# Rows added, measured and normalized, and projection weights mixed, inside the first convolution's edge pass

## The chip, the cores and the metric

One core of a Trainium2 chip runs one program that computes the whole network. The metric is the device time of one execution in microseconds, median of several runs. The engines are TensorE (PE, with its weight load PEld), VectorE (DVE), ScalarE (ACT), GpSimd (POOL) and SyncE (SP, which here only issues DMAs).

## What is computed

A graph has 6250 nodes with 256 features and 100000 edges, sorted by destination. First a graph convolution is added to the input and the rows are normalized; then three attention layers with weights by node type and edge type run over the same edges.

```python
h = x @ W
norm = deg_inv_sqrt[src] * deg_inv_sqrt[dst]
out = segment_sum(h[src] * norm[:, None], dst)         # first convolution
x = layernorm(x + out)                                 # rows of the node stage
# attention, layer 0 of 3: K, V, Q of each node, by node type; keys also by edge type
Q = typed(x, W_Q, node_type); K = typed(x, W_K, node_type); V = typed(x, W_V, node_type)
kt = typed(K[src], W_E, edge_type); scores = sum(Q[dst] * kt) / sqrt(HD) * mu.T[edge_type]
```

## The kernel before

The nodes are 50 windows of 128, of which 49 (`FILLED`) hold nodes. The edges are 832 tiles of 128, two tiles are a duo (`PAIRS` = 416), and 16 duos (`RING`) are a turn (`TURNS` = 26). Two stages matter here.

`gcn_edges` is the edge pass of the convolution. For each duo n: GpSimd gathers two tiles of scaled source rows into a ring of 16 duos (`fetch_source`, L802); VectorE makes the one-hot matrix of destinations (`make_hot`, L1045) and, two duos later, copies its transpose to bytes (`copy_columns`, L1055); ScalarE casts the one-hot twice (L925, L926) and evacuates finished sums from PSUM to `g.sums` (L909); TensorE turns the one-hot (L959), multiplies it with the gathered rows (L964) and clears the columns of the next sum (L944). SyncE stores both one-hots and, once a turn, a record that VectorE makes (`record`, L1016 to L1034) after a small product on TensorE (L972) in PSUM bank 3. The first turn is written out, the rest is a hardware loop. Each engine runs its own list in order; semaphores connect them.

Then `end_phase` clears the semaphores and lets all engines meet at a barrier.

`gcn_nodes` is the node stage. SyncE loads x (L1258) and the projection's weights. VectorE adds `dis * sums` to x for a window (L1329), measures it (`bn_stats`, L1335), and for a batch of windows (3, 4, 5, 7, 9, 11, 10) computes scale and shift in `norm_scales` (aggregation L1202, then 13 small dependent steps, the last L1208). ScalarE normalizes a window with these (L1284) and stores each batch to `x_state` (L1288). The projection (class `Projection`) then takes one window after another: GpSimd masks the rows by node type (`mask`, L1522, two buffers), TensorE turns eight blocks (`turn`, L1456), ScalarE copies them (`copy`, L1496), TensorE mixes them with the weights (`mix`, L1466), ScalarE copies values and queries out (`out`, L1504, L1505), VectorE the keys (`keys`, L1549), and SyncE stores both to `kv_table` (L1425, L1426), 780 KB a window. On ScalarE step n is: copy window n, out window n-1, then up to two normalizations of later windows. Before the first mix the key weights are turned (L1442), copied (L1490), mixed with the edge-type weights (L1448) and scaled (L1535). All first additions, scales and weight products stand ahead of the first window.

## Time and profile before

| | us |
|---|---|
| median of 3 runs | 6294.59 (6286.68 to 6299.7) |
| the profiled execution | 6286.31 |
| its span | 6284.6 |
| edge pass of the convolution, in the profile | about 150 to 1190 |
| node stage | 1190 to 1414 |
| TensorE busy over the span | 5335.7 (85%) |
| VectorE | 4540.0 (72%) |
| ScalarE | 2873.6 (46%) |
| GpSimd | 3896.3 (62%) |
| mean granted TensorE clock | 0.944 of full speed |

Times in the profile run from the start of the span. The granted clock of TensorE is given as a share of 2.4 GHz; 0.50 is 1.2 GHz. An idle time in brackets stands before the instruction, with what ended it.

### The profile page before, as it was taken

How to read it: one execution, taken by the hardware profiler on the slowest of the kernel's cores; microseconds unless marked ns; L12 is line 12 of the kernel's file. 1: busy time of each engine (PE TensorE's matmuls, PEld its weight loads, DVE VectorE, ACT ScalarE, POOL GpSimd, SP SyncE). 2: the span in 40 equal slices, each digit the busy share in tenths (PEclk: the TensorE clock that was granted, in tenths of full speed). 3: DMA queues.
4: the chain of work that ended last, by engine and by line, in shares of the span. 5: the costliest groups of instructions: out<-in, count | busy, mean ns of one | idle time of the engine just before them, and what ended most of it. 6: DMA issues, size and time to landing. Idle time of an engine off the chain costs nothing. (4 is left out here: it accounts for less than half of the span.)

```text
span 6284.6 us, 121542 instructions
## 1 busy us (share of the span) xinstructions
PE 5335.7 (85%) x27435; PEld 4203.1 (67%) x27436; DVE 4540.0 (72%) x10955; ACT 2873.6 (46%) x8788; POOL 3896.3 (62%) x3826
## 2 busy tenths in 40 slices
PE   5777776688888888999888888889997888888997
PEld 4444444575666666888766666678895666666786
DVE  6433333457888887665488888876646898888797
ACT  3555544454555554223355555532243555555343
POOL 1777777547777775334577777733356777776343
PEclk8887888898999999999899999999998999999998
DMA  3444444568888885004888888830178888887111
GB/s 124 148 146 146 145 145 146 181 233 261 251 251 249 249 250 178 30 30 140 277 250 251 251 249 248 250 94 30 33 246 264 248 250 251 250 251 216 38 50 39
DMA packets 568576, 1153.38 MB, mean 184 GB/s; under 512 B 86585, under 2 KB 327803, under 8 KB 568427
## 3 DMA queue, kind: packets, MB, share of 16 engines
q0 software_dynamic: 239984, 774.78, 41.8%
q1 hardware_dynamic: 301919, 351.59, 17.0%
q10 hardware_dynamic: 26524, 25.41, 1.2%
q8 instruction: 45, 0.74, 0.0%
q14 instruction: 104, 0.85, 0.0%
HBM read 960.31 MB, written 191.18 MB: 183 GB/s over the span
## 5 line engine op out<-in xcount | busy, mean ns | idle before, releaser
L1742 POOL DMA_INDIRECT at_kv<-kv_table,idx_kv x1664 | 1579.7, 949 | 554.0 <-issue 455.9
L1758 ACT COPY sums<-ps x2499 | 949.5, 380 | 1517.1 <-PE ps L1869 1490.4
L1833 PE MATMUL ps<-at_wv,at_hot 128*128 128x264 f32 x3328 | 1039.2, 429 | 170.0 <-DVE at_wv L1941 64.4
L802 POOL DMA_INDIRECT gc_rows<-x_scaled,idx_x x832 | 793.1, 953 | 341.0 <-issue 248.0
L1742 POOL DMA_INDIRECT at_kv_last<-kv_table,idx_kv x832 | 789.8, 949 | 273.5 <-issue 220.8
L1869 PE MATMUL ps<-sums,at_hot_t 128*128 x3328 | 885.3, 390 | 23.5 <-DVE at_prod L1923 17.7
L964 PE MATMUL ps<-gc_rows,gc_hot 128*128 128x256 f32 x1664 | 669.1, 526 | 215.9 <-DMA gc_rows<-x_scaled,idx_x 214.6
L1833 PEld LDWEIGHTS ps<-at_wv,at_hot 128*128 128x128 f32 x3328 | 504.0, 191 | 401.2 <-DVE at_wv L1941 157.1
L1869 PEld LDWEIGHTS ps<-sums,at_hot_t 128*128 128x128 f32 x3328 | 619.9, 194 | 123.7 <-ACT at_hot_t L1787 19.2
L1923 DVE TENSOR_TENSOR at_prod<-ps,at_kv 128x512 f32<-128x512 f32 x832 | 572.6, 688 | 154.2 <-DMA at_kv<-kv_table,idx_kv 130.5
L1941 DVE TENSOR_TENSOR at_wv<-ps,at_kv 128x528 f32<-128x528 f32 x832 | 581.4, 699 | 98.7 <-ACT ps L1796 97.0
L1055 DVE CAST gc_hot_t<-ps 128x256 uint8<-128x256 f32 x416 | 176.2, 424 | 616.2 <-PE ps L964 616.2
L1833 PE MATMUL ps<-at_wv_last,at_hot_last 128*128 128x264 f32 x1664 | 519.6, 429 | 85.5 <-DVE at_wv_last L1941 32.0
L1964 DVE TENSOR_REDUCE at_score<-at_prod 128x16 f32<-128x512 f32 x832 | 562.9, 677 | 0.7
L964 PEld LDWEIGHTS ps<-gc_rows,gc_hot 128*128 128x128 f32 x1664 | 323.6, 242 | 342.7 <-DMA gc_rows<-x_scaled,idx_x 265.9
L909 ACT COPY sums<-ps x833 | 310.1, 372 | 481.0 <-PE ps L964 463.9
L1869 PE MATMUL ps<-sums,at_hot_t_last 128*128 x1664 | 442.2, 390 | 13.0 <-DVE at_prod_last L1923 10.4
L1817 PE MATMUL ps<-zeros_b 128*128 128x8 bf16 x2496 | 422.5, 169 | 0.0
L1833 PEld LDWEIGHTS ps<-at_wv_last,at_hot_last 128*128 128x128 f32 x1664 | 252.1, 191 | 201.4 <-DVE at_wv_last L1941 76.3
L1787 ACT CAST at_hot_t<-at_hot_t 128x256 f32<-128x256 uint8 x832 | 345.0, 415 | 38.7 <-PE ps L1869 38.6
L1869 PEld LDWEIGHTS ps<-sums,at_hot_t_last 128*128 128x128 f32 x1664 | 310.2, 194 | 61.6 <-issue 10.9
L2176 PE MATMUL ps<-an_x1t,nw_w 128*128 128x256 f32 (+1 forms) x1600 | 347.6, 375 | 1.3 <-ACT an_x1t L2228 1.3
(420 smaller groups left out, 10213.5 us busy)
## 6 DMA issues: line engine op xcount, KB each, us to landing
kv_table<-pj_v_next SPq DMA_DIRECT2D x98, 396.0 KB, 3.6
kv_table<-pj_k_next SPq DMA_DIRECT2D x98, 384.0 KB, 2.8
at_hot_t<-hot_columns SPq DMA_DIRECT2D x104, 256.0 KB, 4.2
at_kv<-kv_table,idx_kv POOLq DMA_INDIRECT x1664
at_hot<-hot_rows SPq DMA_DIRECT2D x104, 256.0 KB, 4.9
at_rec<-block_records SPq DMA_DIRECT2D x104, 226.0 KB, 3.7
kv_table<-pj_v SPq DMA_DIRECT2D x49, 396.0 KB, 3.3
kv_table<-pj_k SPq DMA_DIRECT2D x49, 384.0 KB, 2.7
```

What stands on the lines that cost most here:

```text
L802: nc.gpsimd.indirect_dma_start(g.gcn_rows[:, (2 * k + j) * D:(2 * k + j + 1) * D], None, g.xs_d, bass.IndirectOffsetOnAxis(index, 0)).then ...
L964: mm = t.matmul(at[j], hot[:, k, j, :], rows[:, (2 * k + j) * D:(2 * k + j + 1) * D], start=False, stop=True, skip_group_check=True)
L1742: nc.gpsimd.indirect_dma_start(kv[:, 2 * k + j, :], None, g.tab_d.rearrange("t n c -> (t n) c"), bass.IndirectOffsetOnAxis(index, 0)).then ...
L1758: act.copy(dest, source).then_inc(evacuated, 1)
L1787: act.copy(hot_t[:, slot % HRING].rearrange("p j e -> p (j e)"), hot_t8[:, b, u, :]).then_inc(t_cast, 1)
L1817: return t.matmul(columns, g.zeros_b[:, 0:P], g.zeros_b[:, 0:RESET], start=True, stop=True, skip_group_check=True)
L1833: mm = t.matmul(own[j], hot[:, slot % HRING, j, :], wv[:, slot % WRING, j, :], start=False, stop=True, skip_group_check=True)
L1869: mm = t.matmul(ps[:, slot % Q_BANKS, j * D:(j + 1) * D], hot_t[:, slot % HRING, j, :], q_rows[j], start=True, stop=True)
L1923: v.tensor_tensor(prod[:, slot % 2].rearrange("p (j c) -> p j c", j=2), ps[:, slot % Q_BANKS, :].rearrange("p (j c) -> p j c", j=2), keys, ...
L1941: v.tensor_tensor(wv[:, slot % WRING].rearrange("p j (h e) -> p j h e", h=HEADS), weight[:, 2 * w:2 * w + 2, :, None].to_broadcast([P, 2, ...
L1964: v.tensor_reduce(score[:, par, 2 * w:2 * w + 2, :], prod[:, slot % 2].rearrange("p (j h e) -> p j h e", j=2, h=HEADS), AX.X, ALU.add).the ...
L2176: mm = t.matmul(ps[:, 3 + f // 2, (f % 2) * 2 * P:(f % 2 * 2 + wins) * P], w1[:, c, f * P:(f + 1) * P], x1t[:, c, 0:wins].rearrange("p w n ...
```

## The change

The projection's weights and the first 35 windows of x are loaded during turns 1 to 6 of the edge pass. In the last 21 duos (395 to 415) VectorE adds and measures one window each and makes the scales of three batches of seven; ScalarE normalizes one window in each of the steps 404 to 417, 14 in all. The key weights are turned, copied, mixed and scaled in halves in duos 397 to 407, in PSUM bank 3. The last two turns are written out instead of looped so that this can stand in them. Two batches are stored by SyncE at the end of the pass. The node stage begins with the first mask at once, normalizes the other 35 windows in batches of 7, 7 and 14 as it goes, and puts four of the projection's buffers where the ring of gathered rows was. The edge pass and the constants:

```diff
 BRING = 4
 
 
-def gcn_edges(nc, g):
+GCN_BATCHES = (7, 7, 7, 7, 7, 14)
+GCN_IN_PASS = 3
+X_LOT = 7
+EARLY_LOTS = 5
+assert sum(GCN_BATCHES) == FILLED and FILLED % X_LOT == 0
+GCN_STARTS = [sum(GCN_BATCHES[:k]) for k in range(len(GCN_BATCHES) + 1)]
+GCN_LISTS = [range(a, b) for a, b in zip(GCN_STARTS, GCN_STARTS[1:])]
+READY_BY = E // P + 1
+FIRST_PREPARED = (READY_BY + 8) // 2
+TURN_HALVES, MIX_HALVES, SCALE_HALVES = (397, 400), (403, 405), (405, 407)
+COPY_HALVES = (399, 402)
+FIRST_NORMED = FIRST_PREPARED + GCN_BATCHES[0] + 2
+GCN_NORMED = PAIRS + 2 - FIRST_NORMED
+PEELED = 2
+assert RING * (TURNS - PEELED) <= min(FIRST_PREPARED, TURN_HALVES[0]) and FIRST_PREPARED + GCN_STARTS[GCN_IN_PASS] == PAIRS
+assert GCN_STARTS[2] <= GCN_NORMED < GCN_STARTS[3]
+
...
@@ -874,6 +893,10 @@
                                  hot_t8[:, b].rearrange("p u e -> p (u e)")).then_inc(hot_t8_stored[b], 16)
 
                 def turn(i, last=False):
+                    if isinstance(i, int) and i == 1:
+                        gn.pj.load_weights(sp)
+                    if isinstance(i, int) and 2 <= i < 2 + EARLY_LOTS:
+                        gn.load(sp, i - 2)
                     store_hots(i, 0)
                     need_apart(sp, rec_ready, i + 1)
                     sp.dma_start(g.rec_d[bass.ds(2 * i, 2)].rearrange("b p r -> p b r"), rec[:]).then_inc(stored, 16)
@@ -882,10 +905,13 @@
                     store_hots(i, 1)
 
                 load_keys(0)
-                turn(0)
-                with sp.Fori(1, TURNS - 1) as i:
+                for i in range(2 + EARLY_LOTS):
+                    turn(i)
+                with sp.Fori(2 + EARLY_LOTS, TURNS - 1) as i:
                     turn(i)
                 turn(TURNS - 1, last=True)
+                for k in range(2):
+                    gn.store(sp, k)
                 for b in range(2):
...
@@ -926,10 +952,16 @@
                             act.copy(hot8[:, b, u, :], hot[:, k].rearrange("p j n -> p (j n)")).then_inc(hot8_made, 1)
                         if not isinstance(n, int) or n >= 1:
                             evacuate(n - 1, 0, words, w + 1)
+                        if isinstance(n, int) and n in COPY_HALVES:
+                            gn.pj.copy_half(act, CROSS_BANK, COPY_HALVES.index(n))
+                        if isinstance(n, int) and n >= FIRST_NORMED:
+                            gn.normalize(act, n - FIRST_NORMED)
 
                 act.wait_ge(cleared, 1)
                 turn(0)
-                with act.Fori(1, TURNS) as i:
+                with act.Fori(1, TURNS - PEELED) as i:
+                    turn(i)
+                for i in range(TURNS - PEELED, TURNS):
...
@@ -967,8 +999,15 @@
                                 mm.then_inc(summed, 1)
                             need(t, evacuated, 2 * n + j + 3 - SUM_BANKS)
                             restart(after[j])
+                        if isinstance(n, int) and n in TURN_HALVES:
+                            t.wait_ge(rec_ready, i + 1 if k > AT_RECORD else i)
+                            gn.pj.turn_half(t, CROSS_BANK, TURN_HALVES.index(n))
+                        if isinstance(n, int) and n in MIX_HALVES:
+                            gn.pj.mix_half(t, CROSS_BANK, MIX_HALVES.index(n))
                         if k == AT_CROSS:
                             t.wait_ge(ends_ready, i + 1)
+                            if isinstance(i, int) and i == TURNS - 1:
+                                t.wait_ge(gn.pj.w_ready, 2)
                             t.matmul(g.ps[:, CROSS_BANK, 0:2 * CROSS], g.same_head[:], ends[:].rearrange("p q c -> p (q c)"),
...
@@ -1059,15 +1100,23 @@
                         make_hot(i, k)
                         if k >= LAG_COPY:
                             copy_columns(i, k - LAG_COPY)
-                        elif not isinstance(i, int):
+                        elif not isinstance(i, int) or i > 0:
                             copy_columns(i - 1, RING + k - LAG_COPY)
                         if k == AT_ENDS:
                             tile_ends(i)
                         if k == AT_RECORD:
                             record(i)
+                        n = RING * i + k
+                        if isinstance(n, int) and n in SCALE_HALVES:
+                            gn.pj.scale_half(v, CROSS_BANK, SCALE_HALVES.index(n))
+                        if isinstance(n, int) and n >= FIRST_PREPARED:
+                            v.wait_ge(evacuated, READY_BY + n - FIRST_PREPARED)
+                            gn.prepare(v, n - FIRST_PREPARED)
 
                 turn(0)
-                with v.Fori(1, TURNS) as i:
+                with v.Fori(1, TURNS - PEELED) as i:
+                    turn(i)
+                for i in range(TURNS - PEELED, TURNS):
                     turn(i)
                 for k in range(RING - LAG_COPY, RING):
```

The rows and the node stage, cut to what matters (`load` is called by SyncE in both stages):

```diff
-GCN_BATCHES = (3, 4, 5, 7, 9, 11, 10)
-    return min(FILLED, sum(GCN_BATCHES[:2]) + (5 * (n + 1) + 3) // 4)
+    return min(FILLED, GCN_STARTS[GCN_IN_PASS] + 3 + (n + 1))
...
+        self.late = {"pj_xm": 0, "pj_xmt": 2 * HEADS * P, "pj_k": 4 * HEADS * P, "pj_v": 4 * HEADS * P + 2 * EDGE_TYPES * D}
+        self.g = g
+        self.y = sb("gn_y", [P, EARLY_LOTS * X_LOT, D])
+        self.m = MomentTiles(sb, "gn", max(GCN_BATCHES))
...
+    def load(self, sp, k):
         whole = N // P
+        some = range(X_LOT * k, min(X_LOT * (k + 1), whole))
+        sp.dma_start(self.those(some), windows_in(self.g.x, some)).then_inc(self.x_in[k], 16)
+        if X_LOT * (k + 1) > whole:
+            sp.wait_ge(self.y_cleared, 1)
+            sp.dma_start(self.row(whole)[0:N - whole * P], self.g.x[whole * P:N, :]).then_inc(self.x_in[k], 16)
+
+    def store(self, eng, k):
+        some = GCN_LISTS[k]
+        eng.wait_ge(self.normed, some[-1] + 1)
+        eng.dma_start(windows_in(self.g.x_d, some), self.those(some)).then_inc(self.stored, 16)
+
+    def normalize(self, act, win):
+        k = gcn_batch(win)
+        at_scale = win - GCN_LISTS[k][0]
+        if at_scale == 0:
+            act.wait_ge(self.scales_ready, k + 1)
+        act.activation(self.row(win), self.row(win), ACT.Identity, bias=self.m.shift[:, k % 2, at_scale:at_scale + 1],
+                       scale=self.m.rstd[:, k % 2, at_scale:at_scale + 1]).then_inc(self.normed, 1)
+
+    def prepare(self, v, win):
+        g, y, k = self.g, self.row(win), gcn_batch(win)
+        if win % X_LOT == 0:
+            v.wait_ge(self.x_in[win // X_LOT], 16 * (2 if win + X_LOT == FILLED else 1))
+        sums = g.sums[:, UROW * (win + 1):UROW * (win + 1) + D]
+        v.scalar_tensor_tensor(out=y, in0=sums, scalar=g.dis[:, win:win + 1], in1=y,
+                               op0=ALU.mult, op1=ALU.add).then_inc(self.added, 1)
+        if win not in GCN_STARTS:
+            self.statistics(v, win - 1)
+        if win == GCN_LISTS[k][-1]:
+            self.statistics(v, win)
+
+    def statistics(self, v, win):
+        m, k = self.m, gcn_batch(win)
+        v.wait_ge(self.added, win + 1)
+        d = v.bn_stats(m.stat[:, win - GCN_LISTS[k][0], :], self.row(win))
+        if win == GCN_LISTS[k][-1]:
+            d.then_inc(self.vec, 1)
+            self.signals += 1
+            v.wait_ge(self.vec, self.signals)
+            need(v, self.normed, GCN_LISTS[k - 2][-1] + 1 if k >= 2 else 0)
+            norm_scales(v, m, k % 2, slice(0, len(GCN_LISTS[k])), self.vec, self.signals, self.scales_ready)
+            self.signals += SCALE_SIGNALS - 1
+
+
+def gcn_nodes(nc, g, gn):
+
+    pj, normed, added = gn.pj, gn.normed, gn.added
+    with nc.sbuf_tensor("gn_y_late", [P, FILLED - EARLY_LOTS * X_LOT, D], F32) as gn.y_late,             nc.Block(no_gpsimd_drain=True) as block:
+
+        @block.sync
+        def _(sp):
+            for k in range(EARLY_LOTS, FILLED // X_LOT):
+                gn.load(sp, k)
+            pj.store_all(sp)
+            sp.wait_ge(gn.stored, 16 * len(GCN_LISTS))
+
+        @block.tensor
+        def _(t):
+            pj.multiply_first(t)
+            pj.multiply(t)
+
+        @block.scalar
...
+        @block.scalar
+        def _(act):
+            done = GCN_NORMED
+            act.wait_ge(pj.ones_set, 1)
+            for n in range(FILLED):
+                pj.copy(act, n, n % 2)
+                if n >= 1:
+                    act.wait_ge(added, min(n + 1, FILLED))
+                    pj.out(act, (n - 1) // 2, (n - 1) % 2)
+                for win in range(done, min(done + 2, gcn_scaled(n - 2))):
+                    gn.normalize(act, win)
+                    done = win + 1
+                    if win + 1 in GCN_STARTS:
+                        gn.store(act, gcn_batch(win))
+                assert done >= min(n + 4, FILLED)
+            pj.out(act, pj.TURNS - 1, 0)
+
...
+            v.memset(gn.row(N // P), 0.0).then_inc(gn.y_cleared, 1)
+            done = GCN_STARTS[GCN_IN_PASS]
+            for n in range(-1, FILLED):
+                if n >= 0:
+                    pj.keys(v, n)
+                for win in range(done, gcn_prepared(n)):
+                    gn.prepare(v, win)
+                    done = win + 1
+
...
+    def turn_half(self, t, bank, half):
+        t.wait_ge(self.k_in, 16 * (NODE_TYPES + 2))
+        need(t, self.kt_copied, half)
+        for k in range(4):
+            tr = t.transpose(self.g.ps[0:HD, bank, k * P:(k + 1) * P], self.wk[:, 4 * half + k, :], self.g.ident[:])
+        tr.then_inc(self.kt_turned, 1)
+
+    def copy_half(self, act, bank, half):
+        act.wait_ge(self.kt_turned, half + 1)
+        act.copy(self.wkt[:, 4 * half:4 * half + 4, :].rearrange("p h n -> p (h n)"),
+                 self.g.ps[0:HD, bank, :]).then_inc(self.kt_copied, 1)
+
+    def mix_half(self, t, bank, half):
+        t.wait_ge(self.kt_copied, 2)
+        need(t, self.w_ready, half)
+        for k in range(4):
+            mm = t.matmul(self.g.ps[:, bank, k * EDGE_TYPES * HD:(k + 1) * EDGE_TYPES * HD],
+                          self.wkt[:, 4 * half + k, :], self.we[:, :, 4 * half + k, :], start=True, stop=True)
+        mm.then_inc(self.w_mixed, 1)
+
+    def scale_half(self, v, bank, half):
+        if half == 0:
+            v.tensor_scalar(self.mu[:], self.mu[:], float(HD) ** -0.5, None, ALU.mult).then_inc(self.mu_scaled, 1)
+            v.wait_ge(self.mu_scaled, 1)
+        v.wait_ge(self.w_mixed, half + 1)
+        v.tensor_tensor(self.w[:, 4 * half:4 * half + 4, 2:PROJ, :],
+                        self.g.ps[:, bank, 0:4 * EDGE_TYPES * HD].rearrange("p (h t e) -> p h t e", h=4, t=EDGE_TYPES),
+                        self.mu[:, 4 * half:4 * half + 4, :, None].to_broadcast([P, 4, EDGE_TYPES, HD]),
+                        ALU.mult).then_inc(self.w_ready, 1)
...
         self.turn(t, 0, 0)
-        t.wait_ge(self.w_ready, 1)
+        t.wait_ge(self.w_ready, self.ready)
         t.wait_ge(self.w_in, 16 * 2 * NODE_TYPES)
```

## Rows read from the trace of the kernel before

**Rows 1.** Stretches: PE, PEld, DVE, ACT, POOL busy, PE clock, DMA share, GB/s.
```profile
1100.00:1150.00 50.00, 34.23 (x164) 22.54 (x165) 19.10 (x60) 26.34 (x84) 37.81 (x41) 0.84 0.50 148
...
1390.00:1400.00 10.00, 10.00 (x81) 10.00 (x80) 3.36 (x10) 5.89 (x22) 5.21 (x3) 1.00 0.79 269
```

**Rows 2.** Lines of 180:1180: busy us, mean ns | idle before us, releasers.
```profile
L802 POOL DMA_INDIRECT gc_rows<-x_scaled,idx_x x797 | 758.3, 951 | 242.8 <-issue 237.9 <-PE ps L964 4.9
L964 PE MATMUL ps<-gc_rows,gc_hot 128*128 128x256 f32 x1607 | 648.3, 527 | 215.7 <-DMA gc_rows<-x_scaled,idx_x 214.4
...
L1055 DVE CAST gc_hot_t<-ps 128x256 uint8<-128x256 f32 x403 | 170.7, 424 | 598.7 <-PE ps L964 598.7
```

**Rows 3.** Order of time, end of the pass: start us, us, instruction [idle before].
```profile
1171.63 0.41 DVE L1016 TENSOR_TENSOR br_rec<-br_kt 128x254 f32<-128x254 f32 x1
...
1173.50 1.04 POOL L802 DMA_INDIRECT gc_rows<-x_scaled,idx_x  x1 [0.31 <-issue]
...
1174.34 0.42 DVE L1045 TENSOR_TENSOR gc_hot<-ps,gc_place 128x256 f32<-128x256 f32 x1
...
1181.10 0.95 POOL L802 DMA_INDIRECT gc_rows<-x_scaled,idx_x  x1 [0.30 <-issue]
...
1185.05 1.20 PE L964 MATMUL ps<-gc_rows,gc_hot 128*128 128x256 f32 x2
...
1186.79 0.33 SPq L873 DMA_DIRECT2D hot_columns<-gc_hot_t  x1
```

**Rows 4.** Order of time, GpSimd at the start of the node stage.
```profile
1190.36 0.13 POOL L1515 MEMSET pj_v<- 128x16 f32 x1 [8.31 <-POOLq L95]
1200.98 3.74 POOL L1522 TENSOR_TENSOR pj_xm<-gn_y,type_hot 128x1024 f32<-128x1024 f32 x2 [10.50 <-ACT gn_y L1284]
```

**Rows 5.** Order of time, TensorE in the node stage.
```profile
1204.10 1.97 PE L1456 MATMUL ps<-ident,pj_xm 128*128 128x128 f32 x8
...
1213.59 1.04 PE L1456 MATMUL ps<-ident,pj_xm 128*128 128x128 f32 x8
...
1287.66 1.97 PE L1456 MATMUL ps<-ident,pj_xm 128*128 128x128 f32 x8 [6.23 <-POOL pj_xm L1522]
1289.42 3.64 PE L1466 MATMUL ps<-pj_w,pj_xmt 128*128 128x160 f32 x16
...
1388.29 1.04 PE L1456 MATMUL ps<-ident,pj_xm 128*128 128x128 f32 x8
...
1391.33 1.04 PE L1456 MATMUL ps<-ident,pj_xm 128*128 128x128 f32 x8
...
1401.36 4.51 PE L1466 MATMUL ps<-pj_w,pj_xmt 128*128 128x160 f32 x32
```

**Rows 6.** Waits in 1177:1415: us in total, times, longest us.
```profile
POOL pj_xm L1522 <- ACT gn_y L1284: 63.0, 7, 11.3
...
ACT sums L1504 <- DMA kv_table<-pj_v: 36.0, 20, 4.6
```

**Rows 7.** Order of time, VectorE in the node stage.
```profile
1227.36 1.09 DVE L1549 COPY pj_k<-ps 128x288 f32<-128x288 f32 x3 [1.84 <-ACT pj_v L1505]
1228.37 0.48 DVE L1329 SCALAR_TENSOR_TENSOR gn_y<-sums,dis,gn_y 128x256 f32<-128x256 f32 x1
...
1232.44 0.17 DVE L1208 SCALAR_TENSOR_TENSOR gn_shift<-gn_mom,gn_rstd 128x5 f32<-128x5 f32 x1
...
1307.98 1.82 DVE L1329 SCALAR_TENSOR_TENSOR gn_y<-sums,dis,gn_y 128x256 f32<-128x256 f32 x1
```

**Rows 8.** Lines of 1177:1415, by form: busy us, mean ns | idle before.
```profile
L1284 ACT ACTIVATE gn_y<-gn_y,gn_shift,gn_rstd 128x256 f32<-128x256 f32 x49 | 27.9, 631 | 14.9 <-DVE gn_shift L1208 14.9
...
L1335 DVE BATCH_NORM_STATS2 gn_stat<-gn_y 128x6 f32<-128x256 f32 x49 | 19.8, 417 | 0.0
...
L1202 DVE BATCH_NORM_AGGREGATE gn_mom<-gn_stat 128x2 f32<-128x6 f32 x49 | 4.0, 154 | 0.2
...
L1448 PE MATMUL ps<-pj_we,pj_wkt 32*128 32x96 f32 x16 | 3.7, 423 | 1.1 <-ACT pj_wkt L1490 1.1
```

More of the change, by code:

```diff
@@ L3 @@
 from contextlib import ExitStack
+import math
 F32 = mybir.dt.float32
@@ L1233, in sem @@
             s = ctx.enter_context(nc.semaphore(name))
[L1234 removed]
+            self.sems.append(s)
             return s
[L1237 to L1244 removed]
```

181 lines of the change are left out of this document (60 added, 121 removed).

## The prediction

> **What bounds the kernel now.** Read the table of stretches first [rows 1]. The change touches two stages: the edge pass of the first convolution (to about 1190 us) and the node stage behind it, with the projection (1190 to 1414 us). In the pass no engine is full; GpSimd is busy 37.8 of 50 us, and the grouped lines of the pass say why that is a limit all the same: each gather takes 951 ns and is followed by about 0.30 us of issue [rows 2], so a gather every 1.25 us and a duo (two gathers) every 2.5 us. TensorE waits 215.7 us for gathered rows in about 403 duos, 0.54 us a duo: it has slack, and so have VectorE (19.1 of 50 us) and ScalarE (26.3 of 50). The order of time at the end of the pass [rows 3] shows TensorE only about one duo behind GpSimd: the last gather is issued at 1181.10 and its rows are multiplied from 1185.05. The ring holds 16 duos, so a late TensorE does not hold GpSimd up; it only matters at the end.
>
> The node stage is the other way round. In its last undisturbed stretch TensorE is busy 10.0 of 10 us at the full clock [rows 1], and a window takes 1391.33 - 1388.29 = 3.04 us (take 3.05) [rows 5]. That is the floor. The stage is far from it for two reasons: a slow start [rows 4] and stalls at each batch of normalizations [rows 5 to 7].
>
> **Part 1, the start.** Before, the stage begins with x loads, three additions, moments, scales and weights: GpSimd is free at 1190.36, but the first mask starts at 1200.98, the first turn of rows on TensorE at 1204.10, and window 2 turns at 1213.59 [rows 4, 5]. After the change 14 windows are normalized and the weights mixed when the stage begins. Without the pass's own delay (part 3) the first mask comes at about 1190.5, 1.9 us long (two take 3.74 [rows 4]), a hand-over of 0.1: first turn at 1192.5, so 11.6 us earlier. From there to window 2 the same chain runs (turn, copy, turn, mix, all at the slower pace: a turn takes 1.97 us there and 1.04 at window 2 [rows 5]), since in both kernels TensorE comes out of an idle stretch: 9.5 us again. Gain 11.6 us.
>
> **Part 2, the stalls.** From 1213.59 (turn of window 2) to the end of the last mix at 1401.36 + 4.51 = 1405.87 [rows 5] is 192.3 us. The floor is 46 windows x 3.05 = 140.3 us to the last turn, 0.9 us from a turn's start to its mix, and the last two mixes, 4.51 us: 145.7 us. So 46.6 us are lost. Five batch stalls leave TensorE idle 3.31, 4.25, 6.23, 3.87 and 4.64 us (the longest, one of five such lines, in [rows 5]), 22.3 us; after four of them TensorE is at that slower pace (1.2 GHz, half) for most of a mix (4.01, 3.64, 4.12, 3.77 us in place of 2.34; one of four lines in [rows 5]) and in three for a turn (1.97 in place of 1.04), 8.9 us more. Together 31.2 us. The remaining 15.4 us are small waits, mostly for ScalarE's copy, which itself waits 36.0 us for stores of the table [rows 6]: the x_state stores get in their way.
> Why five stalls? GpSimd waited 63.0 us for normalized rows and ScalarE 14.9 us for scales [rows 8]. Normalizing is so close ahead of the masks that each batch empties GpSimd, and the chain scale, normalize, mask, turn is then paid in full.
> After: 35 of 49 windows remain to be normalized in the stage (14 done), 28 to be added, in three batches (7, 7, 14). At step n the code has at least n + 4 normalized, and 21 + 7 in hand around each batch, so a mask no longer waits. What stays is ScalarE's own wait: it stands in the queue for the scales of windows 21, 28 and 35, and the copy behind it is what TensorE needs. Its length: for a batch of five VectorE's copy of the keys starts at 1227.36, with ScalarE's output copies nearly through (they end 0.4 us later), and the shift is ready at 1232.61 [rows 7]: 4.8 us from the end of the output copies; with 0.08 us for each more window [rows 8] seven take 5.0, fourteen 5.5; ScalarE arrives one window, 3.05 us, later, so it waits 1.9 to 2.5 us. That is the low bound. High bound: now GpSimd does mask meanwhile, and an addition that meets a mask takes 1.82 us, not 0.48 [rows 7], 1.3 us more, and the first small step of the scales may wait out most of another mask, some 1.2 us: 1.9 + 1.3 + 1.2, about 4.5 us, and as idle times of that size brought the low clock, 2 us more. Two of the three batches come just behind an x_state store, where the masks are through; I take 2.6 + 2.6 + (4.6 + 2.1) = 12 us (the first two between 1.9 and the 3.0 that ScalarE waited on average before, 14.9 us in 5 [rows 8]), bounds 6 and 20.
> The other waits: 15.4 us before, with 6.4 MB of x loads and 6.4 MB of x_state stores inside the stage; after, 1.8 MB of loads and 4.6 MB of stores (two batches are stored by SyncE at the end of the pass, and travel before the first table store). 10 us, bounds 8 and 15. Sum 145.7 + 12 + 10 = 167.7, a gain of 24.6 us.
> On the contention of mask and addition the Trainium skill (SBUF — State Buffer, "Who interferes with whom") has a rule: a VectorE instruction with two inputs in SBUF and a GpSimd instruction that reads SBUF exclude each other for the whole instruction. By that rule the high bound would hold wherever a mask runs; the additions of 1.82 and 0.48 us agree.
>
> **Part 3, what the pass pays.** Each of the last 21 duos gets an addition (0.48 [rows 7]) and a measuring (0.42 [rows 8]): VectorE 0.96 + 0.9 = 1.9 us of 2.5. ScalarE gets a normalization of 0.6 us [rows 8] from duo 404 on: 1.3 + 0.6 = 1.9 of 2.5. Neither becomes a bound by that. Over single duos it is otherwise. Scales of a batch cost 7 x 0.08 + 13 x 0.2 = 3.2 us more in duos 401, 408 and 415, the record in duo 411 costs 2.7 us (from 1171.63 to the next one-hot at 1174.34 [rows 3]), the last halves of the weights in 407 1.5 us with their wait. One-hots are made about two duos ahead, 3.7 us before TensorE would notice, and in duos 401 to 407 that holds. From the sums of duo 405 to the end, ten duos at 2.5 = 25 us, VectorE has: nine duos at 0.84 + 0.9 = 15.7 (a one-hot 0.42 [rows 3], a column copy 0.42 [rows 2]), two chains of scales 6.4, record 2.7, weights 1.5, a last measuring 0.4 and two more column copies 0.8, and some 0.5 of arrears: 28 us. Its last column copy ended 0.45 us after the last sums before; now it comes about 3 us later, and SyncE stores the last columns after it. The barrier comes 3 us later. If TensorE ran at the full clock and VectorE started that stretch without arrears, 2; if every wait adds, 5.
> TensorE's new work is 3.7 us of mixing [rows 8] and about half of that of turning (as many columns in eight blocks, not sixteen) in duos 397 to 405; with 0.54 us a duo of idle time plus the higher clock that full work brings, ten duos take it back. What is queued behind the added waits: behind VectorE's wait for the mixed weights the one-hot of the next duo, which ScalarE and TensorE want; its wait for evacuated sums has been met long before; behind ScalarE's wait for scales (three duos after they are made) the evacuations.
> At the end SyncE then waits for ScalarE's last two normalizations (its last evacuation is done 0.9 us after the last sums, about 1187.2, and 1.2 us follow), and would issue by 1189.2, so this is hidden; the one-hot store issued at 1186.79 [rows 3], for which the barrier waits, has landed by 1190.3, when GpSimd is let on [rows 4]. Loads: 14 for the weights and five lots of 0.9 MB on SyncE's queue in turns 1 to 6, where a turn is 40 us, the queue issues some 12 us at most of this, and the DMA engines are half idle (0.50) [rows 1]; a late gather there is taken back by the ring. The stores of one-hots pass behind them. The peeled turns I cost at 0, since straight-line code of the node stage ran without gaps of its own; bounds 0 and 2. The gathers: beside the record's VectorE work one took 1.04, not 0.95 [rows 3]; 0.09 us for each of two would be 0.18 us for 2.7 us of such work, and the 29 us of additions, measurings and scales about 2 us at that rate, but GpSimd's last gather has 3 us before VectorE's tail, which covers it. Pass in all +3 us, bounds 0 and +5.
>
> **Sum.** 11.6 + 24.6 - 3 = 33 us. The profiled execution has 6284.6 us of span in 6286.3; the median of the three times is 6294.6, 8.3 above, with 13 us between lowest and highest. I take the gain off the median: 6294.6 - 33.2 = 6261.4, say 6261 (6253 against the profiled execution).
>
> **Rivals.** (A) The batch stalls go almost wholly: ScalarE waits only 1.9, 1.9 and 2.5 us, and nothing drops the clock. 145.7 + 6 + 9 = 161; gain 11.6 + 31.6 - 2 = 41, 6253. For: additions beside an idle GpSimd are short. Against: GpSimd is busier now.
> (B) Another wait takes their place. With the start gone, masks and additions meet at every step, VectorE (keys 1.1, addition up to 1.8, measuring 0.4 = 3.3 us) is slower than 3.05, or the table stores pace the stage: losses of 20 + 15 us. 181 us, gain 11.6 + 11.6 - 4 = 19, 6275. For: 36.0 us of waiting for stores. Against: 269 GB/s at a share of 0.79 at the floor [rows 1].
> (C) Slower: the gathers of the last 21 duos are held by VectorE's new work. If each of the 42 gathers waits out an addition and a measuring (0.9 us) and the three chains stand in the way too, 42 x 0.9 + 9.6 = 47 us are lost: 6294.6 - 33 + 47 = 6308. It decides from about 0.8 us for each gather on; at half the price the gain is 10. Against: 1.04 in place of 0.95 is the worst row [rows 3].
> For (C) the Trainium skill (SBUF — State Buffer, "Reading the diagram") says that descriptor generation on GpSimd stops while VectorE runs an operation in a two-port mode; of the new work only the few small tensor-scalar steps could be that.
> (D) The work is moved and the stage does not start earlier, since something else ends its wait at 1204 (stores of the pass on the DMA engines): gain 24.6 - 3 = 22, 6273.
>
> **Chances.** Forecast 0.55, A 0.17, B and D 0.22, C 0.03, other 0.03. 0.2% is 12.6 us, about what a measurement of this kernel can tell. Faster by more 0.91, within 0.05, slower 0.04. Range: A with 8 us of scatter below (the times of before lie 13 us apart), B with 3 above: 6245 to 6278.
>
> **What would show it.** Right: the first mask within 1 us of the stage's beginning, the first turn 2 us behind it; no long wait of GpSimd for normalized rows; three waits of ScalarE for scales of 2 to 5 us; from window 2 to the last mix 162 to 175 us; the last gather still at 1181 to 1183, and the last column copy about 3 us after 1186.7. Wrong: masks waiting for rows, gathers over 1.0 us in the last 50 us of the pass, TensorE still multiplying sums after 1191, or additions of 1.8 us throughout with VectorE late.

## The result and the profile after

| | before | after |
|---|---|---|
| median, us | 6294.0 (6286.68 to 6299.7, 5 runs) | 6259.37 (6252.95 to 6263.97, 5 runs) |
| ratio to before | 1 | 0.9944, interval 0.9933 to 0.9955 |
| span of the profiled execution | 6284.6 | 6251.2 |
| first turn of rows on TensorE | 1204.10 | 1192.66 |
| turn of window 2 | 1213.59 | 1201.03 |
| last mix ends | 1405.87 | 1373.41 |
| window 2's turn to that end | 192.3 | 172.4 |
| first TensorE instruction of the next stage, after that end | 8.90 | 7.66 |

The kernel is 35 us faster. In the traces 33.7 us lie between the start of the pass and the next stage: 12.6 before window 2's turn (and here the pass's own price is in), 19.9 in the stage behind it and 1.2 at its end. Timed again (second group of the experiments), the same change is 31.3 us faster, and there the three parts are 10.1, 19.8 and 1.2: the stage repeats, the end of the pass does not.

The end of the pass, first by stretches (PE, PEld, DVE, ACT, POOL busy, PE clock, DMA share, GB/s), kernel before:

```profile
1150.00:1187.00 37.00, 28.77 (x120) 18.52 (x117) 13.33 (x43) 17.70 (x56) 24.43 (x26) 0.74 0.42 129
```

and kernel after:

```profile
1150.00:1187.00 37.00, 24.63 (x132) 16.75 (x130) 31.43 (x123) 25.10 (x73) 24.77 (x26) 0.90 0.43 131
```

VectorE more than doubles its busy time and GpSimd's does not move. TensorE has more to do and is busy for less time, at a clock of 0.90 and not 0.74; that clock is not the change's doing, since the repeat of the same kernel has 0.77 in this stretch. In order of time, VectorE, GpSimd and SyncE's queue of after (start us, us, instruction, idle before it):

```profile
1175.04 0.41 DVE L1096 CAST gc_hot_t<-ps 128x256 uint8<-128x256 f32 x1
1175.37 0.48 DVE L1348 SCALAR_TENSOR_TENSOR gn_y<-sums,dis,gn_y 128x256 f32<-128x256 f32 x1
1175.76 0.42 DVE L1358 BATCH_NORM_STATS2 gn_stat<-gn_y 128x6 f32<-128x256 f32 x1
1176.10 0.41 DVE L1086 TENSOR_TENSOR gc_hot<-ps,gc_place 128x256 f32<-128x256 f32 x1
1176.42 0.41 DVE L1096 CAST gc_hot_t<-ps 128x256 uint8<-128x256 f32 x1
...
1184.97 0.17 DVE L1257 SCALAR_TENSOR_TENSOR gn_shift<-gn_mom,gn_rstd 128x7 f32<-128x7 f32 x1
...
1186.46 0.42 DVE L1096 CAST gc_hot_t<-ps 128x256 uint8<-128x256 f32 x1 [0.99 <-PE ps L996]
```

```profile
1173.66 1.22 POOL L803 DMA_INDIRECT gc_rows<-x_scaled,idx_x  x1 [0.30 <-issue]
...
1181.44 0.95 POOL L803 DMA_INDIRECT gc_rows<-x_scaled,idx_x  x1 [0.30 <-issue]
1190.64 0.12 POOL L1613 MEMSET gc_rows<- 128x16 f32 x1 [8.25 <-POOLq L96]
1190.72 3.92 POOL L1620 TENSOR_TENSOR gc_rows<-gn_y,type_hot 128x1024 f32<-128x1024 f32 x2
```

```profile
1186.97 0.33 SPq L892 DMA_DIRECT2D hot_columns<-gc_hot_t  x1
```

The last gather is 0.34 us later than in [rows 3] (the first gather of the pass already starts 0.32 us later, at 136.12 and not 135.80), the last one-hot store 0.18, GpSimd's first instruction of the stage 0.28 later than in [rows 4]. VectorE even waits 0.99 us for TensorE before its last column copy; in the repeat it does not. The masks run at once, in place of 10.5 us of waiting.

TensorE of after in the node stage, in order of time (against [rows 5]):

```profile
1192.66 1.97 PE L1554 MATMUL ps<-ident,gc_rows 128*128 128x128 f32 x8 [6.23 <-POOL gc_rows L1620]
...
1197.61 3.58 PE L1564 MATMUL ps<-pj_w,gc_rows 128*128 128x160 f32 x16
1201.03 1.04 PE L1554 MATMUL ps<-ident,gc_rows 128*128 128x128 f32 x8
...
1221.45 1.94 PE L1554 MATMUL ps<-ident,gc_rows 128*128 128x128 f32 x8 [4.54 <-ACT gc_rows L1594]
1223.18 4.44 PE L1564 MATMUL ps<-pj_w,gc_rows 128*128 128x160 f32 x16
...
1301.51 1.94 PE L1554 MATMUL ps<-ident,gc_rows 128*128 128x128 f32 x8 [4.68 <-ACT gc_rows L1594]
1303.24 3.67 PE L1564 MATMUL ps<-pj_w,gc_rows 128*128 128x160 f32 x16
...
1330.91 1.07 PE L1554 MATMUL ps<-ident,gc_rows 128*128 128x128 f32 x8 [1.62 <-ACT gc_rows L1594]
...
1368.90 4.51 PE L1564 MATMUL ps<-pj_w,gc_rows 128*128 128x160 f32 x32
```

Five batch stalls have become three (the middle one is 4.59 us at 1251.43). Behind each a turn takes 1.94, which is the 1.2 GHz level, and a mix 3.1 to 4.4 where it is 2.34 at full clock, so the mix is at that level nearly throughout or in part. Behind the idle time of 1.62 a turn takes 1.07. Who waits, in 1188:1412 of after (engine, line and releaser: us in total, times, longest), against [rows 6]:

```profile
POOL gc_rows L1620 <- PE ps L1554: 81.4, 47, 6.8
...
ACT sums L1602 <- DMA kv_table<-gc_rows: 21.2, 12, 3.8
...
ACT gn_y L1340 <- DVE gn_shift L1257: 7.3, 2, 4.2
...
ACT gn_y_late L1340 <- DVE gn_shift L1257: 4.6, 1, 4.6
```

GpSimd no longer waits for normalized rows at all (63.0 us before), only for TensorE to take the last mask. ScalarE waits 11.9 us for scales, in three waits, and 21.2 us for table stores, not 36.0. What makes the scales so late is seen on VectorE and GpSimd of after at the first batch:

```profile
1212.06 2.06 DVE L1348 SCALAR_TENSOR_TENSOR gn_y<-sums,dis,gn_y 128x256 f32<-128x256 f32 x1
1214.05 0.75 DVE L1358 BATCH_NORM_STATS2 gn_stat<-gn_y 128x6 f32<-128x256 f32 x2
1214.83 0.58 DVE L1251 BATCH_NORM_AGGREGATE gn_mom<-gn_stat 128x2 f32<-128x6 f32 x7
1215.44 1.42 DVE L1254 TENSOR_SCALAR gn_var<-gn_mom 128x7 f32<-128x7 f32 x1
```

```profile
1211.95 1.89 POOL L1620 TENSOR_TENSOR gc_rows<-gn_y,type_hot 128x1024 f32 x1 [1.53 <-PE ps L1554]
1214.94 1.89 POOL L1620 TENSOR_TENSOR gc_rows<-gn_y,type_hot 128x1024 f32 x1 [1.09 <-PE ps L1554]
```

The addition ends 0.28 us after one mask (which ends at 1213.84), and a step on seven numbers ends with the next (the mask at 1216.83, the step at 1216.86): 1.42 us in place of 0.17. The measuring falls into the gap between the two masks; the aggregating reaches into the second one and keeps its length. The same step took 1.55 and 1.09 us in the other two batches.

### The profile page after: what moved, and what is told of

It reads as the page before. It is cut to its first block and busy times, and to the rows that moved or that the text cites. A ratio compares the mean times of both kernels' runs of the same rounds, so it can differ in the third digit from the quotient of the medians.

```text
span 6251.2 us, 121147 instructions
## 1 busy us (share of the span) xinstructions
PE 5329.7 (85%) x27435; PEld 4199.9 (67%) x27436; DVE 4542.2 (73%) x10942; ACT 2874.4 (46%) x8789; POOL 3894.5 (62%) x3826
```

## Experiments

Kernels of one group ran on one chip, beside the kernel before: 6281.48 us there in the first group (9 runs, 6278.02 to 6286.09), 6283.89 in the second (9 runs), 6289.56 in the third (7 runs), 6282.56 in the last (9 runs). Single times carry no interval; so the traces' stage (window 2's turn to the end of the last mix) carries the argument. Edits are against the kernel after where nothing else is said.

### First group: where the gain comes from, what the stalls are

**The wait moved away from the copies.** ScalarE takes its normalizations two steps later, so that scales are ready when it asks.

```diff
-                for win in range(done, min(done + 2, gcn_scaled(n - 2))):
+                for win in range(done, min(done + 2, gcn_scaled(n - 4))):
```

> The kernel after, with one edit: ScalarE takes a batch's first normalization two steps later (it asks for what was scaled at step n - 4, not n - 2). Theory (queue head): the three stalls of the node stage (TensorE idle 4.54, 4.59, 4.68 us, then 6.9 us at the slower pace) exist only because ScalarE stands before its scales with the next copy behind it; two steps are 6.1 us, more than the waits of 3.1, 4.2 and 4.6 us. Then no wait for scales is left and the time from window 2's turn to the end of the last mix falls from 172.4 to 151 to 155 us; the whole 17 to 21 us below the kernel after, near 6240. Rival (VectorE): the chain of 5 us holds VectorE's copy of keys, which the mix behind it needs; then TensorE still idles 1 to 4 us at each batch, and 160 to 168 us are left.

Measured: 6248.02 us (5 runs), ratio 0.9947 (0.9933 to 0.9961); stage 171.7 us. The ratio is that of the change itself. Waits of this kernel in 1188:1412:

```profile
PE ps L1564 <- DVE gc_rows L1647: 11.9, 3, 4.5
```

ScalarE's wait for scales is gone, and TensorE waits 11.9 us for VectorE (in after its three idle times come to 13.8): the chain of scales stands ahead of the copy of the keys, whose bank the next mix needs. That ScalarE's queue alone made the stalls was wrong, and the stage is longer than the rival expected too; VectorE's own queue holds nearly the same time.

**Half a mask.** GpSimd masks four of eight heads, so half of the projection's input is left out.

```diff
-        shape = [P, HEADS, NODE_TYPES, HD]
+        few = HEADS // 2 if self.q_with_v else HEADS
+        shape = [P, few, NODE_TYPES, HD]
```

> The kernel after; GpSimd masks only four of the eight heads of each window in the node stage (half of its columns stay as they were, so that part is not computed), a mask of about 0.95 us. Theory (contention): additions and the first step of the scales wait out masks; with masks half as long ScalarE's three waits for scales (3.1, 4.2, 4.6 us) fall by 1.2 to 2 us each, towards the 1.9 to 2.5 us of the bare chain, the first small step of the scales (1.42, 1.55, 1.09 us) falls under 0.7, and the stage is 4 to 8 us shorter. Rival (chain alone): the waits stay within 0.5 us of what they are, since the lengths of VectorE's own steps make them.

Measured: 6246.73 us (one run), stage 168.1 us, 4.3 below after. At the first batch, VectorE in order of time:

```profile
1212.32 1.21 DVE L1348 SCALAR_TENSOR_TENSOR gn_y<-sums,dis,gn_y 128x256 f32<-128x256 f32 x1
...
1214.83 0.17 DVE L1254 TENSOR_SCALAR gn_var<-gn_mom 128x7 f32<-128x7 f32 x1
...
1215.24 1.02 DVE L129 TENSOR_SCALAR gn_rstd<-gn_bits 128x7 int32<-128x7 int32 x1
```

The addition is 0.85 us shorter, and the hold has moved to another step; the three idle times of TensorE are 3.27, 3.12 and 3.63 us in place of 4.54, 4.59 and 4.68. ScalarE's three waits for scales are 1.79, 2.71 and 3.57 us. Contention with the mask is worth at least 4 us of the stage; since half of each mask is left and still holds a step, how the rest of a stall divides between holds and the bare chain is not shown.

**Weights or rows left in the stage.** First the weights' products put back at the start of the stage, rows as in after:

```diff
-                        if isinstance(n, int) and n in MIX_HALVES:
-                            gn.pj.mix_half(t, CROSS_BANK, MIX_HALVES.index(n))
...
+            pj.turn_weights(t)
+            pj.mix_weights(t)
```

> The kernel after without the weight part in the pass (turning, copying, mixing and scaling of the key weights stand at the start of the node stage as before; their loads stay in the pass). Theory: the start then pays turn 1.9, copy 1.5, mix 3.7 us ahead of the first turn of rows, which comes at 1198 in place of 1192.7, and window 2 about 4 us later than 1201.0 (TensorE has been busy longer, so its clock may rise sooner and give 1 us back). Rival: the rows' masks set the start and the weights hide beside them: under 1.5 us later. The end of the pass moves by under 0.5 us in both.

Measured: 6253.93 us (one run), first turn at 1197.96, window 2 at 1205.58, stage 171.7: 5.3 us later at the start (4.6 at window 2; 4.6 also counted from GpSimd's first instruction, which is itself 0.7 later in this trace) and nothing after it.

Then the rows: x and weights loaded early and the weights mixed in the pass, but nothing added or normalized there. The stage then works by the old schedule of additions, in batches of 3, 4, 5, 7, 9, 7 and 14.

```diff
-GCN_BATCHES = (7, 7, 7, 7, 7, 14)
+GCN_BATCHES = (3, 4, 5, 7, 9, 7, 14)
...
-                        if isinstance(n, int) and n >= FIRST_PREPARED:
-                            v.wait_ge(evacuated, READY_BY + n - FIRST_PREPARED)
-                            gn.prepare(v, n - FIRST_PREPARED)
```

> The other half alone: x and the weights are loaded and the weights mixed in the pass, but no row is added, measured or normalized there; the stage works in batches of 3, 4, 5, 7, 9, 7, 14 with the old schedule. Theory (head start of rows): batch stalls are back, since masks again wait for normalized rows: GpSimd waits 45 to 65 us for them, from window 2 to the last mix 185 to 192 us, and the first turn of rows comes at about 1198. The x loads' absence from the stage is worth the little rest, 2 to 6 us. Rival (traffic): the 6.4 MB of x loads in the stage were what made the stalls; then the stage takes 175 us or less although nothing is prepared.

Measured: 6271.62 us (one run), first turn at 1198.42, window 2 at 1206.47, stage 191.6 us, which is that of the kernel before (192.3). Its waits in 1188:1412:

```profile
POOL gc_rows L1614 <- ACT gn_y L1329: 44.1, 6, 11.1
...
ACT sums L1596 <- DMA kv_table<-gc_rows: 20.8, 13, 3.6
POOL gc_rows L1614 <- ACT gn_y_late L1329: 16.7, 2, 11.1
```

GpSimd again waits 60.8 us for normalized rows, and TensorE has five stalls again. The length is that of before, but its parts are not. The stalls cost 24.5 us of idle time (2.69, 4.25, 6.21, 4.54, 6.82) and 12.7 us of lower clock behind them, 37.2 in all where the prediction counted 31.2 before; the batches differ. The small waits are 191.6 - 145.7 - 37.2 = 8.7 us and were 15.4, and ScalarE's wait for table stores is 20.8 us, as in after. So loading x early goes with 6.7 us less of small waits, hidden here by longer stalls. The head start of rows takes the masks' waits away, brings the stalls from 37.2 down to 20.7 us and is what shortens the stage. It was the mechanism of part 2.

### Second group: what the pass pays, and how VectorE's order decides

**The change again**, as the base of this group.

> The kernel after unchanged, so that it and its variants are timed on one chip. Both theories: 31 to 36 us below the kernel before, stage and start as in the profile of after within 1 us.

Measured: 6252.61 us (5 runs, 6245.98 to 6253.59), ratio 0.9948 (0.9934 to 0.9961), 31.3 us below the kernel before; stage 172.5, first turn at 1194.50. The stage is the same within 0.1 us, and the start of it 1.8 us later. The end of the pass in this trace:

```profile
1150.00:1187.00 37.00, 29.35 (x135) 19.84 (x133) 28.63 (x110) 25.26 (x73) 24.73 (x26) 0.77 0.43 131
```

```profile
1184.94 0.68 PE L996 MATMUL ps<-gc_rows,gc_hot 128*128 128x256 f32 x2
...
1187.86 0.17 DVE L1257 SCALAR_TENSOR_TENSOR gn_shift<-gn_mom,gn_rstd 128x7 f32<-128x7 f32 x1
1187.95 0.75 DVE L1096 CAST gc_hot_t<-ps 128x256 uint8<-128x256 f32 x2
...
1192.49 0.13 POOL L1613 MEMSET gc_rows<- 128x16 f32 x1 [10.13 <-POOLq L96]
```

TensorE's last sums end at 1185.62, sooner than in the first trace (1186.42). But VectorE's last chain of scales runs until 1188.0, and the last two column copies stand behind it: they end at 1188.70, 3.1 us behind the sums, and 2.0 us later than in the kernel before. The last one-hot store and the stage follow from there. So the pass costs 2.1 us here at GpSimd's first instruction (1192.49 against 1190.36), and not 0.3. Ten traces of this document have exactly this pass, two of the change and eight of kernels that alter only the node stage. In two of them the last column copy waits for TensorE and ends 0.46 us behind the sums, as in the kernel before; in eight it stands behind the scales and ends 1.1 to 3.1 us behind them. GpSimd's first instruction comes at 1189.61 to 1193.31, 1191.3 in the mean, 1.0 us later than in the one trace of the kernel before. TensorE's clock between 1150 and 1187 us is 0.72 to 0.90 over the ten; what makes one execution differ from the next is not shown.

**Each window measured three times in the pass**, to see what VectorE's time there costs.

```diff
+        if win < GCN_STARTS[GCN_IN_PASS]:
+            for again in range(2):
+                v.bn_stats(self.extra[:, 2 * win + again, :], self.row(win))
```

> The kernel after with each of the 21 measurings in the edge pass done three times (the two extra ones into a tensor nobody reads). Theory (VectorE was nearly full in the last ten duos, and the prediction's 28 us counted durations of overlapping instructions): two more cost 0.68 us a duo from start to start, and with about 1.3 us of idle time left the last column copy comes 5 to 7 us later than 1186.9, while TensorE's last sums come 1 to 4 us later. Rival (VectorE had plenty of room): under 2 us later. By the prediction's way of counting it would be 11 us.

Measured: 6255.3 us (one run), stage 172.4. The end of VectorE's pass:

```profile
1185.26 0.74 DVE L1361 BATCH_NORM_STATS2 gn_extra<-gn_y 128x6 f32<-128x256 f32 x2
...
1187.30 0.74 DVE L1361 BATCH_NORM_STATS2 gn_extra<-gn_y 128x6 f32<-128x256 f32 x2
...
1192.48 0.75 DVE L1096 CAST gc_hot_t<-ps 128x256 uint8<-128x256 f32 x2
```

Duos now follow each other by 2.04 us on VectorE without a gap, each two measurings of 0.33 us longer, and the column copies end at 1193.2, 6.3 us after those of after and 4.5 after those of its repeat, 4.8 us behind TensorE's last sums; the first turn is 6.4 and 4.5 us later. So more work on VectorE at the end of the pass is paid for in time. The change itself stands at the edge: in some executions it pays nothing for its own, in others up to 2.6 us (3.08 behind the sums less 0.46).

**The addition ahead of the keys**, so that it runs when no mask does; alone, and with normalizing two steps later.

```diff
-                if n >= 0:
-                    pj.keys(v, n)
-                for win in range(done, gcn_prepared(n)):
-                    gn.prepare(v, win)
+                some = range(done, gcn_prepared(n))
+                keys = (lambda: pj.keys(v, n)) if n >= 0 else None
+                if keys is not None and not len(some):
+                    keys()
+                for win in some:
+                    gn.prepare(v, win, keys)
+                    keys = None
```

> The addition ahead of the keys alone, ScalarE's normalizations as in after. Theory: the chain starts about 1.1 us sooner, so ScalarE's three waits fall from 3.1, 4.2, 4.6 to 2 to 3.5 us; additions mostly take 0.5 to 1.0 us, not 1.5. The stage is 165 to 170 us. Rival: an addition ahead of the keys meets the mask just as well and holds the keys in every step; then additions stay near 1.5 us and the stage is 173 us or more.

Measured: 6243.08 us (one run), stage 168.3, TensorE's idle times 3.14, 3.38 and 3.85.

> The late normalization of the run before and, in the node stage, each window's addition on VectorE ahead of the copy of keys, not behind it. Theory (VectorE is the owner of the stall): with normalizations late, the mix waits for keys that stand behind addition, measuring and chain (about 6.6 us from the keys' usual end). The addition ahead of the keys falls into the gap between two masks and takes about 0.5 us more of VectorE's idle time, so keys stand only 5 us late at a batch; two banks give 3 us of slack: TensorE's three idle times fall from 3.7, 3.7 and 4.5 to 1 to 2.5 us, the low clock after them goes in at least two, and the stage is 158 to 165 us, not 171.7. Rival (the chain's length alone decides): the three idle times stay over 3.3 us, since the chain itself is unchanged.

Measured: 6239.43 us (5 runs, 6236.84 to 6241.13), ratio 0.9928 (0.9914 to 0.9941), stage 163.0. Its additions take 1225 and 1106 ns in the mean, after's 1442 and 1437. Waits in 1188:1412:

```profile
ACT sums L1607 <- DMA kv_table<-gc_rows: 36.2, 16, 6.6
...
PE ps L1569 <- DVE gc_rows L1652: 5.7, 3, 3.7
```

TensorE's waits for the keys are down to 1.0, 1.0 and, at the batch of 14, 3.7, and no turn runs at the lower clock. Later normalizing alone gave nothing (0.7 us), the order alone 4 us, both 9: at the first batch VectorE takes 9.8 us from one copy of the keys to the next with later normalizing alone (1212.38 to 1222.21) and 7.1 us here (1210.11 to 1217.24), and so the slack of two steps covers most of it.

### Third group: can the stalls go altogether

**Batches of seven only**, on top of the kernel above.

```diff
-GCN_BATCHES = (7, 7, 7, 7, 7, 14)
+GCN_BATCHES = (7, 7, 7, 7, 7, 7, 7)
```

> Addition first and late, batches of seven, the scales in one piece. Theory: the wait of 3.69 us at the batch of 14 becomes two of about 1 us, those at the others stay near 1.05, each without the low clock: stage 160 to 163 us. Rival (each chain in one piece costs the same whatever its list): a fourth chain more, 163 to 167 us.

Measured: 6242.74 us (one run), stage 161.4. The wait of 3.7 is gone; three waits for keys of 1.0 us and four of 1.4 for ScalarE's copy remain.

**The chain of scales spread**, on top of the addition ahead of the keys: the 14 steps of a batch's scales five at a time behind the keys, and ScalarE asks for what was scaled at step n - 5.

```diff
+    def advance(self, v, count):
+        for _ in range(min(count, len(self.pending))):
+            step = self.pending.pop(0)
+            v.wait_ge(self.vec, self.signals)
...
-                for win in range(done, min(done + 2, gcn_scaled(n - 4))):
+                for win in range(done, min(done + 2, gcn_scaled(n - 5))):
...
+                gn.advance(v, 5)
```

> Addition first and late normalizations as before (ScalarE now asks for what was scaled at step n - 5); seven batches of 7; and VectorE takes the 14 steps of a batch's scales five at a time behind the keys of three windows, not all at once. Theory (VectorE's block of 5 us in one piece is what TensorE waits for): no mix waits over 0.5 us for keys at a batch, no turn after window 2 at the slower pace; what is left are waits behind x_state stores, 1.4 to 1.6 us four or five times. Stage 152 to 158 us (163.0 in the run before), the whole 5 to 10 us below that run, about 45 to 54 below the kernel before. Rival (VectorE is full anyway: keys 1.0, addition up to 1.8, measuring 0.35 in 3.05 us): spread over windows the same work keeps it late, and the stage stays at 160 to 164 us.

> The same with the batches 7, 7, 14 in the stage. Theory: the longer list only lengthens one aggregation to 1.1 us; within 2 us of the kernel with seven batches, the store of 1.8 MB costing one longer wait (1.5 to 4 us) in place of two short ones. Rival: the batch of 14 is what is left of the stalls: 3 us or more slower than with sevens.

Measured, sevens: 6230.19 us (4 runs, 6228.91 to 6231.04), ratio 0.9907 (0.9891 to 0.9924), stage 152.6. Batches of 7, 7, 14: 6224.52 (one run), stage 152.7.

> The kernel of e10_spread once more, now timed in rounds against the kernel before, since its one time (6224.52 us) carries no interval: the addition ahead of the keys, rows normalized five steps later, the 14 steps of a batch's scales taken five at a time behind the keys, batches of 7, 7 and 14 in the stage. By the traces of e10_spread and e11_spread_sevens both stages take 152.6 to 152.7 us from window 2's turn to the last mix's end, so the batch's size no longer matters, and the 4.4 us between their spans is the start of the stage (1.2) and work behind it. If that is right, the stage is 151.5 to 154 again, no low TensorE clock falls into it, and the ratio to the kernel before is 0.988 to 0.992, with e11_spread_sevens' 0.9907 inside the interval's reach. If the batches of 14 really save the 5.7 us between the two times, the ratio is 0.9895 or below and the stage no longer than 152.7. A stage of 158 or more would say that one trace each was luck.

Measured, the same kernel in five rounds: 6230.52 us (6227.94 to 6231.6), ratio 0.9918 (0.9904 to 0.9931), stage 152.66. The single time of 6224.52 was low for this kernel (its first turn at 1191.62 against 1194.19 is 2.6 of the 6.0 us), and the size of the batch no longer matters. VectorE's chain of this last kernel, and its stage by stretch:

```profile
1215.89 0.17 DVE L1372 TENSOR_TENSOR gn_half<-gn_var,gn_rstd 128x7 f32<-128x7 f32 x1
1215.98 0.48 DVE L1349 SCALAR_TENSOR_TENSOR gn_y<-sums,dis,gn_y 128x256 f32<-128x256 f32 x1
1217.43 1.08 DVE L1687 COPY gc_rows<-ps 128x288 f32<-128x288 f32 x3 [0.98 <-ACT gc_rows L1643]
1218.44 0.15 DVE L1373 SCALAR_TENSOR_TENSOR gn_half<-gn_half,gn_rstd 128x7 f32<-128x7 f32 x1
```

```profile
1203.00:1355.00 152.00, 147.78 (x1142) 144.52 (x1140) 96.55 (x261) 102.91 (x368) 85.17 (x45) 1.00 0.81 278
```

The keys come in the middle of the chain, TensorE is busy 147.8 of 152 us at the full clock, and what is left above the floor of 145.7 is 7 us. This kernel beats the one before and the change: its interval lies just below that of the change in either of the latter's two comparisons.

## Why the prediction was right, and where its terms were off

The forecast was 6261 and the change measures 6259.4: a gain of 33.2 us forecast, 34.6 measured, 31.3 in the repeat. Its mechanisms held, the sizes of its terms less so, and that the sum is so near is in part luck, since the misses cancel. In the first trace the pass was 2.7 us too dear, the run to window 2 (1.1) and the tail (1.2) were not counted as gains, and the stage's gain was 4.7 too large (24.6 for 19.9). In the repeat the pass was 0.9 too dear and the run to window 2 gave 0.5; the rest is the same.

**The start (part 1): right.** Predicted 11.6 us; from GpSimd's first instruction on, the first turn comes 11.7 us sooner. The run from there to window 2 was taken as 9.5 us again and is 8.4: the first copy wait is 1.25 and not 1.54, and the first mix takes 3.58, not 4.41, so the clock rose sooner. In the repeat it is 9.0, with a mix of 4.21. Counted from GpSimd's first instruction too, leaving the weights in the stage gives 4.6 us of the start back and leaving the rows 6.7, nearly all of the 11.7 between them.

**The stage (part 2): mechanism right, two sizes off.** Predicted 167.7, measured 172.4. No mask waits for rows, as foreseen, and without the head start the stage is 191.6. The term of the stalls was 12 and is 20.7: idle 4.54 + 4.59 + 4.68 = 13.8, and the lower clock behind all three, 3 x 0.90 of turns and 2.10 + 0.78 + 1.33 of mixes, 6.9. That is just above the high bound of 20. The step that failed is the choice between its bounds, "two of the three batches come just behind an x_state store, where the masks are through": in all three batches the first small step was held by a mask (1.42, 1.55, 1.09), and the three additions ahead of them took 2.06, 1.58 and 1.69. A mask starts when TensorE has taken the one before, so it has a fixed place beside the keys, whatever is stored. Working with an average of five waits of before, 3.0, was the second half of the mistake: those were waits beside an idle GpSimd. The other term, small waits, was 10 and is 172.4 - 145.7 - 20.7 = 6.0, below its bounds of 8 to 15. The experiment without rows, with x loaded early, has 8.7 us of them: that fits the prediction's view that x traffic made part of the 15.4, though no run moved the loads alone.

**The pass (part 3): mechanism right, size too large.** Predicted +3, measured 0.3 at GpSimd's first instruction in the first trace, 2.1 in the repeat and 1.0 in the mean of the ten traces with this pass. "VectorE has 28 us of work in 25" added durations. But in the rows at 1175.04 to 1176.42 each instruction starts before the one ahead has ended: the distances are 0.33, 0.39, 0.34 and 0.32, where the durations say 0.41, 0.48, 0.42 and 0.41. A duo is 1.38 us, not the 1.74 that the prediction took, nine are 12.4, not 15.7, and the sum is 24.7 us in 25. That does not make the price nothing: the last batch's scales, 3 us, stand ahead of the last two column copies, and in the repeat, where VectorE waits for TensorE three times in the duos before (0.68, 1.14 and 0.42 us; once, 1.03, in the first trace), they come behind the last sums. The prediction rightly expected the last column copy there; it missed that this needs no full VectorE, and comes in some executions and not in others. The kernel that measures three times has a duo of 2.04 us, 1.38 and twice 0.33. That the Trainium skill says the same of profiled durations (Perfetto Trace Analysis, "Optimizing Scalar/DVE Operations": the half of the latency that acknowledges the write overlaps with the next instruction) was not used; the 0.08 to 0.09 us of overlap here agree with it. The gathers were priced rightly: of 33 from 1140 us on, three took 1.19 to 1.22 us and the others 0.95, where the kernel before has two of 1.01 and 1.04, and the last one slips by 0.34 us.

**The tail: not foreseen.** From the end of the last mix to the next stage TensorE is idle 7.66 us and not 8.90. ScalarE waited 2.46 and 1.38 us for table stores before its last output copies, and waits once, 1.64, after; those copies end 2.3 us behind the last mix before and 1.35 after, which is 1.0 of the 1.24 us. All kernels of the experiments have 7.6 to 7.7, that without rows too. Which part of the change does it was not tried.

**The rivals.** (A), stalls almost gone: not here, but the spread chain shows that it was to be had, 20 us further. (B) had its sign in the additions (1.44 us in the mean) and was wrong on the consequence: VectorE keeps up between batches, and only the chain makes it late. (C): gathers do not wait. (D): the start did come earlier.

The holds agree with the Trainium skill (SBUF — State Buffer, "Who interferes with whom") also where the rival did not look: it counts tensor-scalar operations among those that can take the pair of ports that VectorE and GpSimd share, and the 1.42 us for seven numbers are one. The measuring, with one input, is not held: in the kernel with the addition first and later normalizing two measurings run inside a mask and take their 0.75 us.

```profile
1211.00 1.89 POOL L1625 TENSOR_TENSOR gc_rows<-gn_y,type_hot 128x1024 f32 x1 [1.53 <-PE ps L1559]
```

```profile
1211.11 0.75 DVE L1360 BATCH_NORM_STATS2 gn_stat<-gn_y 128x6 f32<-128x256 f32 x2
```

## What to carry to other kernels

Sum VectorE's work by the distance between starts, not by durations, when the question is whether it fits; then look at what stands directly ahead of the instruction that the barrier waits for. A price of 2 us can't be read from one trace where the end of a stage moves by as much between executions of one kernel. A wait at the head of one queue that is moved away shows up at the next queue that holds the same time; ask first how long the producer's chain is and what stands in its queue behind it, then cut that chain into pieces with the urgent copy between them. When an operation's price has two values according to what runs beside it, find what fixes its place in time before choosing between them.

## What the runs showed of the hardware

- A VectorE step on 128x7 numbers (0.17 us alone) takes up to 1.86 us when GpSimd's mask is under way; it ends when the mask does, within 0.04 us. Additions of 128x256 that begin beside a running mask end 0.27 to 0.29 us after it. In the kernel with later normalizing:

```profile
1220.04 1.85 DVE L132 SCALAR_TENSOR_TENSOR gn_half<-gn_half,gn_rstd 128x7 f32<-128x7 f32 x1
```

- Steps without a dependence overlap by 0.08 to 0.09 us; dependent ones, with a wait between them, follow each other by 0.20 us at 0.17 us each and don't.
- Over the last 37 us of the pass TensorE's granted clock was 0.90 in one execution of the change and 0.77 in another, 0.74 in the kernel before and 0.86 with no rows in the pass: a difference of this size between two traces says nothing about the kernels.
- The length of an idle time alone did not tell the clock behind it. Behind 3.73 us a mix took 4.60 us (later normalizing), behind 3.69 us it took 2.41 (addition first and later normalizing), and behind 2.69 us a turn took 1.83 (without rows).
